# A gated cross-attention and feed-forward block: key maxima by differences and relu, and a changed store of keys

## The reference

```python
q = (query @ Wq + bq).reshape(Bq, Sq, H, DK)
k = (key @ Wk + bk).reshape(Bq, Sk, H, DK)
v = (value @ Wv + bv).reshape(Bq, Sk, H, DK)
scores = jnp.einsum('bqhd,bkhd->hbqk', q, k) / np.sqrt(DK)
attn = jax.nn.softmax(scores.reshape(H * Bq, Sq, Sk), axis=0).reshape(H, Bq, Sq, Sk)
out = jnp.einsum('hbqk,bkhd->bqhd', attn, v).reshape(Bq, Sq, H * DK)
...
xq = _act_fake_quant(x, clip_x[0])
gate = jnp.einsum('bsh,ih->bsi', xq, _weight_fake_quant(w_gate))
up = jnp.einsum('bsh,ih->bsi', xq, _weight_fake_quant(w_up))
h = _act_fake_quant(jax.nn.silu(gate) * up, clip_down[0])
return jnp.einsum('bsi,hi->bsh', h, _weight_fake_quant(w_down))
```

## Time and profile before

| what | us |
|---|---|
| median of 3 runs (lowest, highest) | 846.55 (845.84, 848.11) |
| the profiled execution, its own time | 846.44 |
| its span in the trace | 844.6 |
| busy: PE, DVE, ACT, POOL | 737.2, 753.2, 680.6, 468.8 |

### The profile page before, as it was taken

One profiled execution on the slowest core, in us unless ns is written; L12 is line 12 of the kernel. 1 busy time (PEld: TensorE's weight loads), 2 busy tenths in 40 slices (PEclk: granted clock), 3 DMA queues, 4 the chain that ended last, 5 costly groups with the idle time before them and its releaser, 6 DMA issues. The chain is left out here.

```text
span 844.6 us, 19960 instructions
## 1 busy us (share of the span) xinstructions
PE 737.2 (87%) x8129; PEld 446.0 (53%) x8151; DVE 753.2 (89%) x735; ACT 680.6 (81%) x1094; POOL 468.8 (55%) x210
## 2 busy tenths in 40 slices
PE   8898897787777769999999999999999999469977
PEld 6564372111212125676767777777677678424344
DVE  4799738999999978999999999999999995749957
ACT  3454449999999979898999999999999925759873
POOL 1233454000000010999999999999999996414500
PEclk9999999999999989999999999999999999879989
DMA  9774489999997627678867786878877894000014
GB/s 291 235 230 132 143 194 249 277 256 276 253 253 169 236 74 238 181 203 272 267 185 218 247 294 201 231 212 279 252 207 206 253 300 139 0 2 1 1 50 150
DMA packets 94987, 165.88 MB, mean 196 GB/s; under 512 B 10160, under 2 KB 37552, under 8 KB 94384
## 3 DMA queue, kind: packets, MB, share of 16 engines
q1 hardware_dynamic: 94896, 164.60, 67.3%
HBM read 142.81 MB, written 42.73 MB: 220 GB/s over the span
## 5 line engine op out<-in xcount | busy, mean ns | idle before, releaser
L1030 POOL TENSOR_TENSOR e<-e,recip 128x2048 f32<-128x2048 f32 (+2 forms) x113 | 361.4, 3238 | 22.0 <-DVE recip L1063 21.9
L980 ACT ACTIVATE e<-psY 128x512 f32<-128x512 f32 x512 | 296.1, 645 | 30.5 <-PE psY L912 26.0
L1050 DVE TENSOR_REDUCE partial<-e 128x128 f32<-128x4096 f32 (+1 forms) x80 | 279.4, 3559 | 7.1 <-ACT e L980 7.1
L912 PE MATMUL psY<-arena 128*128 128x128 bf16 x2048 | 200.6, 221 | 0.8 <-DMA arena<-k_stack 0.8
L912 PEld LDWEIGHTS psY<-arena 128*128 128x128 bf16 x2048 | 149.2, 98 | 74.6 <-issue 26.3
L707 ACT ACTIVATE copies<-ps_max 128x1024 bf16<-128x1024 f32 x189 | 175.4, 1084 | 0.1
L908 PE MATMUL psY<-shift,minus 128*128 128x512 bf16 x396 | 152.9, 386 | 11.4 <-PEq L641 5.5
L723 DVE TENSOR_TENSOR high<-copies,high 128x3072 bf16<-128x3072 bf16 x63 | 109.9, 1745 | 0.4 <-ACT copies L707 0.4
L1019 POOL MEMSET ones_w<- 96x128 bf16 x1 | 0.2, 207 | 172.6 <-POOLq L641 172.6
L929 PE MATMUL psX<-e,arena 128*32 128x128 f32 x2048 | 75.9, 288 | 4.0 <-issue 1.9
L718 DVE TENSOR_TENSOR high<-ps_max,high 128x1024 bf16<-128x1024 f32 x63 | 76.4, 1213 | 1.5 <-PE ps_max L686 1.5
(11 more groups left out here) (170 smaller groups left out, 1003.4 us busy)
## 6 DMA issues: line engine op xcount, KB each, us to landing
arena<-k_stack SPq DMA_DIRECT2D x264, 256.0 KB, 3.4
arena<-q_stack SPq DMA_DIRECT2D x64, 256.0 KB, 4.3
arena<-in_x_dram SPq DMA_DIRECT2D x8, 1024.0 KB, 10.0
k_stack<-parts SPq DMA_DIRECT2D x24, 256.0 KB, 3.1
q_stack<-parts SPq DMA_DIRECT2D x24, 256.0 KB, 3.1
k_stack<-k_stack SPq DMA_DIRECT2D x4, 1536.0 KB, 20.6
q_stack<-q_stack SPq DMA_DIRECT2D x4, 1536.0 KB, 17.1
arena<-in_ctx_dram SPq DMA_DIRECT2D x4, 1024.0 KB, 5.8
```

Source lines behind the costliest of these rows:

```text
L912: last = nc.tensor.matmul(bank[:, j * P:(j + 1) * P], ks[:, i % KRING, b * P:(b + 1) * P], qs[:, h, b * P:(b + 1) * P], start=False, stop= ...
L980: nc.scalar.activation(e_at(p, half * HB, (half + 1) * HB).rearrange("p q z i -> p z q i"), ps[n % SCORES][:].rearrange("p (z q i) -> p z ...
L1030: nc.gpsimd.tensor_tensor(part, part, by_pairs(recip[:, r % 2, :], share), ALU.mult).then_inc(pool_scaled, 1)
L1050: nc.vector.tensor_reduce(partial[:, :, k, :], e[:, t:t + n].rearrange("p t q z i -> p q i t z"), AX.XY, ALU.add).then_inc(sum_done, 1)
```

## The change

- **Two heads in one product.** The weights and biases of the odd heads' keys get a minus sign (`permute` with signs; on DVE a column `sign` made from `ident`, multiplied into `bk_s`), so that keys of odd heads lie in DRAM negated. A mixed key tile holds the even head's rows above and the negated odd head's below for chunks 0 to 2: one product with the couple's query tile is the difference of the two heads' scores. A group is now one sequence of one couple, again 64 in all. For chunks 0 to 2 ACT takes the relu of the difference (`gain`), and PE computes minus the odd score minus that, which is minus the larger of the two (`ps_y`). DVE takes the minimum of it over all groups straight into `lowest`, 512 and 1024 columns. Chunk 3 stays as it was: two products (`ps_c`), a copy by ACT, and one merge of 1024 columns a group on DVE.
- **Keys in DRAM.** `k_stack` has 5 rows; SyncE writes all five from the parts (three in the last chunk, where one copy makes the others). The copies of keys are gone. A key tile of `attend` is rows 0 to 3 and rows 1 to 4, in two transfers of 128 KB.
- **Loads.** `load_couple` loads both heads of a couple in 14 transfers; for the first couple all 14 stand ahead of the last writes of `prepare`.
- **`attend`**: the matmul of the maximum takes `plus` for even heads and `minus` for odd; the exponential of odd heads has scale -1/4.
- **`ffn`**: item 42 of 44 goes from POOL to DVE. In down, block 0 is rounded, clipped and multiplied by token tiles, `row` is computed behind the clips, and the last block leaves in three pieces, its last tile in another PSUM slot.

```diff
-K_WRITTEN = (0, 1, 2)
+K_WRITTEN = (0, 1, 2, 3, 4)
+K_AT_LAST = (0, 1, 2)
...
-WRITES = len(K_WRITTEN)
-K_COPIED = (((3, 6), (0, 3)), ((6, 8), (0, 2)))
...
+def load_keys(sp, k_stack, kc, h, tile, loaded):
+    at = 0
+    for first, n in K_READ:
+        sp.dma_start(tile[at:at + n * DK], k_stack[kc, h, first * DK:(first + n) * DK, :]).then_inc(loaded, 16)
...
-    if odd is not None:
-        rows(odd[HALF:P], k_stack, 2 * p + 1, K_MAX_ROWS)
+    rows(mixed[0:HALF], k_stack, 2 * p, K_MAX_ROWS)
+    rows(mixed[HALF:P], k_stack, 2 * p + 1, K_MAX_ROWS, NC - 1)
+    for j in range(2):
+        rows(both[j * HALF:(j + 1) * HALF], q_stack, 2 * p + j, Q_MAX_ROWS)
+    rows(odd[HALF:P], k_stack, 2 * p + 1, K_MAX_ROWS)
...
+            c, g = u // GROUPS, u % GROUPS
+            if group(c, g)[0]:
+                return Q_WRITTEN
+            return K_WRITTEN if c < NC - 1 else K_AT_LAST
...
-                        stack, written = ((k_stack, K_WRITTEN), (q_stack, Q_WRITTEN))[m]
+                        stack = (k_stack, q_stack)[m]
                         h0 = dc * (H // DC)
-                        for part, r in enumerate(written):
...
                     act.wait_ge(s[loaded], 16)
-                    nc.scalar.activation(w_p[:].rearrange("p c (e d h) -> p (c e) d h", e=DC, d=DK),
-                                         w_s[:].rearrange("p c (e h d) -> p (c e) d h", e=DC, d=DK),
-                                         ACT.Copy).then_inc(s["w_permuted"], 1)
-                permute(wk_p, wk_s, "wk_loaded")
+                    step = len(signs)
...
+                nc.vector.tensor_reduce(sign[:, 0:1], ident[:, 1:P:2], AX.X, ALU.max).then_inc(s["sign_set"], 1)
+                dve.wait_ge(s["sign_set"], 1)
+                nc.vector.tensor_scalar(sign[:, 1:2], sign[:, 0:1], -2.0, 1.0, ALU.mult, ALU.add
+                                        ).then_inc(s["sign_set"], 1)
...
+                nc.vector.tensor_scalar(bk_s[:], bk_s[:], sign[:, 1:2], None, ALU.mult).then_inc(s["bias_signed"], 1)
...
+        gain = es.enter_context(nc.sbuf_tensor("gain", [P, RING, MIXED, S], BF16))
+        copies = es.enter_context(nc.sbuf_tensor("copies", [P, RING, 2, 2, S], BF16))
...
+        ps_x = es.enter_context(nc.psum_tensor("ps_x", [P, MIXED, S], F32))
+        ps_y = es.enter_context(nc.psum_tensor("ps_y", [P, MIXED, S], F32))
+        ps_c = es.enter_context(nc.psum_tensor("ps_c", [P, 2, S], F32))
...
+                        sp.wait_ge(y_scored, MIXED * B * (p - 1))
...
+                        load_couple(sp, p, k_stack, q_stack, k_mixed[p % 2], k_odd[p % 2], q_pair[p % 2], loaded[p % 2])
...
+                copy_last_keys(sp, k_stack, keep["k_copied"])
...
+                    for kc in range(MIXED):
+                        if g:
+                            pe.wait_ge(gained, 2 * (g - 1) + (2 if kc == MIXED - 1 else 1))
+                        nc.tensor.matmul(ps_x[:, kc, :], keys(k_mixed, g, kc), queries(g), start=True, stop=True
+                                         ).then_inc(x_scored, 1)
...
+                    if g:
+                        pe.wait_ge(c_copied, g)
+                    for j, tile in enumerate((k_mixed, k_odd)):
+                        last_mm = nc.tensor.matmul(ps_c[:, j, :], keys(tile, g, MIXED), queries(g), start=True, stop=True)
+                    last_mm.then_inc(c_scored, 1)
...
+                    for kc in range(MIXED):
+                        if g:
+                            pe.wait_ge(y_merged, 2 * (g - 1) + (1 if kc == 0 else 2))
+                        nc.tensor.matmul(ps_y[:, kc, :], keys(k_odd, g, kc), queries(g), start=True, stop=False)
+                        pe.wait_ge(gained, 2 * g + (2 if kc == MIXED - 1 else 1))
+                        nc.tensor.matmul(ps_y[:, kc, :], minus[:], gain[:, g % RING, kc, :], start=False, stop=True
+                                         ).then_inc(y_scored, 1)
+                for g in range(GROUPS):
+                    differences(g)
+                    plain(g)
+                    if g:
+                        smaller(g - 1)
+                smaller(GROUPS - 1)
...
+                for g in range(GROUPS):
+                    if g >= RING:
+                        act.wait_ge(y_scored, MIXED * (g - RING + 1))
+                    for k0, k1 in ((0, MIXED - 1), (MIXED - 1, MIXED)):
+                        act.wait_ge(x_scored, MIXED * g + k1)
+                        nc.scalar.activation(gain[:, g % RING, k0:k1, :], ps_x[:, k0:k1, :], ACT.Relu
+                                             ).then_inc(gained, 1)
...
+                    act.wait_ge(c_scored, g + 1)
+                    if g % 2 == 0 and g // 2 > RING:
+                        act.wait_ge(c_merged, 2 * (g // 2 - RING))
+                    dst = copies[:, g // 2 % RING, :, g % 2, :] if g >= 2 else last[:, :, g, :]
+                    nc.scalar.activation(dst, ps_c[:], ACT.Copy).then_inc(c_copied, 1)
...
+                    if j == 0:
+                        dve.wait_ge(c_copied, 2 * m + 2)
+                    if m > 1:
+                        dve.wait_ge(c_merged, 2 * (m - 2) + j + 1)
+                    nc.vector.tensor_tensor(last[:, j], copies[:, m % RING, j], last[:, j], (ALU.max, ALU.min)[j]
+                                            ).then_inc(c_merged, 1)
...
+                    for n, (k0, k1) in enumerate(((0, 1), (1, MIXED))):
+                        dve.wait_ge(y_scored, MIXED * g + k1)
+                        if g:
+                            dve.wait_ge(y_merged, 2 * (g - 1) + n + 1)
+                            nc.vector.tensor_tensor(lowest[:, k0:k1, :], ps_y[:, k0:k1, :], lowest[:, k0:k1, :], ALU.min
+                                                    ).then_inc(y_merged, 1)
...
+                    if g > 2:
+                        merge((g - 1) // 2, (g - 1) % 2)
+                merge(GROUPS // 2 - 1, 1)
...
+                dve.wait_ge(c_merged, merges)
+                for j, op in enumerate((ALU.max, ALU.min)):
+                    nc.vector.tensor_tensor(folds[:, j, :], last[:, j, 0, :], last[:, j, 1, :], op).then_inc(c_merged, 1)
+                dve.wait_ge(c_merged, merges + 2)
+                nc.vector.scalar_tensor_tensor(out=lowest[:, MIXED, :], in0=folds[:, 0, :], scalar=-1.0, in1=folds[:, 1, :],
+                                               op0=ALU.mult, op1=ALU.min).then_inc(folded, 1)
...
                         nxt = (i + KRING) % STEPS
-                        sp.dma_start(ks[:, nxt % KRING, :], k_stack[nxt // H, nxt % H]
-                                     ).then_inc(k_loaded[nxt % KRING], 16)
...
                     else:
-                        nc.tensor.matmul(bank[:], minus[:], shift_at(qc, kc).to_broadcast([P, HB, P]),
...
-                                ACT.Exp, scale=DK ** -0.5).then_inc(exped, 1)
+                                ACT.Exp, scale=(DK ** -0.5, -DK ** -0.5)[half // 2]).then_inc(exped, 1)
...
-                return k % PAIR_ITEMS in POOL_I
+                return k % PAIR_ITEMS in POOL_I and k != ITEMS - 2
...
...
+            def place(n, t0, t1):
+                slot = LAST_SLOT if n == NB - 1 and t0 == TB - 1 else n % 4
+                return psD[:, slot, t0 * D:t1 * D]
+            ENDS = ((0, 2), (2, 3), (3, 4))
...
-                    for n in range(NB):
+                    for t in range(TB):
+                        nc.scalar.activation(hi[:, 0:IC, tokens(t)], hs[:, 0:IC, tokens(t)], ACT.Copy,
+                                             scale=h_scale[:, 2:3]).then_inc(s["h_rounded"], 1)
...
+                    for t in range(TB):
+                        dve.wait_ge(s["h_rounded"], t + 1)
+                        nc.vector.tensor_scalar(hq[:, 0:IC, tokens(t)], hi[:, 0:IC, tokens(t)], -QMAX - 1.0, QMAX,
+                                                ALU.max, ALU.min).then_inc(s["hq_ready"], 1)
+                    nc.vector.tensor_scalar(row[:], wd_row[:], h_scale[:, 1:2], tanh_g[:, 1:2], ALU.mult, ALU.mult
+                                            ).then_inc(row_ready, 1)
...
+                    for part, (t0, t1) in enumerate(ENDS):
+                        scaled(NB - 1, part, t0, t1)
+                        summed(NB - 1, part, t0, t1)
...
+                            if t + 1 == TB or n == NB - 1 and t:
+                                last.then_inc(s["down_ready"], 1)
```

More of the change, by code:

```diff
@@ L142, in prepare @@
         ident = sb("ident", [P, P])
-        ident_b = sb("ident_b", [P, P], BF16)
+        ident_b = keep["plus"]
+        sign = sb("sign", [P, 2])
         diag = sb("diag", [P, DC, P])
@@ L230, in v_turn, with rows_written, writes @@
             return B // 2 + i // 2 if c == 1 and i % 2 else None
+        def rows_written(u):
+            c, g = u // GROUPS, u % GROUPS
+            if group(c, g)[0]:
+                return Q_WRITTEN
+            return K_WRITTEN if c < NC - 1 else K_AT_LAST
+        def writes(i, u):
```

(29 more changed lines are left out.)

259 lines of the change are left out of this document (112 added, 147 removed).

## The result

The changed kernel takes **870.62 us** (median of 4 runs, 870.51 to 874.03) against 847.21 for the kernel before in the same comparison: ratio 1.031, 95% interval 1.028 to 1.035. It is slower by 23 us. The forecast was 830.6 with a range of 824.5 to 842.0, so it had the sign wrong.

A forecast was written before the change was run, and what follows sets the result against it. Bounds: ACT and DVE full in `maxima`; DVE, PE and POOL nearly full in `attend`; PE busiest in down. 846.44 + 3.0 + 1.0 + 0.3 - 19.5 + 0.5 + 0.1 - 1.3 = 830.5, median 830.6; range 824.5 to 842.

The forecast's parts named there:

- The key tile in two transfers: In `attend`: same 256 KB a tile, second transfer issued at least 0.32 later, a few more late tiles; +0.5 us, 0 to +8.
- the allowance: In `attend`: four steps of 5.87 us less about 1 while the tile is scored leave 4.87 for a key tile.
- the landing: In `attend`: key tiles landed in 2.4 to 5.7 us, median 3.3; 3.3 + 0.4 stays below the allowed 4.87.
- Rival 2: Key halves slow `attend`, running one after the other at a lower rate: 838 or 864 us in total; chance 0.06.
- The group of 2.47: In `maxima`: waits among PE, ACT and DVE set a group's period at 2.47 us (2.40 to 2.60), saving 19.5.
- the +1.0 of the clock: Start of `maxima`: PE idles some 3 us, then runs at a low granted clock; +1.0 us, 0 to 2.
- the "no cost" of the DMA in `maxima`: In `maxima`: a couple's loads and copies need 13.4 to 15.4 us against 19.8 available, so no cost.
- 0.93 on ACT against 1.13 on DVE: In `maxima`: 1024 f32 columns from PSUM are quicker on ACT; relus on DVE would cost some 100 us.
- End of `prepare`, +3.0: End of `prepare`: four more loads, 0.917 MB, ahead of the last three writes on SyncE's queue; +3.0 us, 2.5 to 5.
- 0.3: In `prepare`: the keys' sign, more and smaller ACT copies, and 12 more key writes of 256 KB; +0.3 us, 0 to 1.5.
- `ffn` and down: Item 42 on DVE and `row` off the path, +0.1 us; down's earlier first product and shorter end, -1.3 (0 to -2).
- -0.5: End of down: the last scale, add (0.69) and write are halves; -0.5 us.

The follow-up runs named there:

- lower half alone: Changed kernel loading only the lower half of each key tile in `attend`, one transfer of 64 partitions, 128 KB (scores not the reference's): 826.50 us.
- lower half and 8 KB to 128 partitions: Changed kernel loading only each key tile's lower half in `attend`, less its last 32 columns, plus a second transfer of 8 KB to all 128 partitions: 845.78 us.
- lower half and 4 KB to 64 partitions: Changed kernel loading only each key tile's lower half in `attend`, plus a second transfer of 4 KB to the upper 64 partitions: 865.97 us.
- before, halves: Kernel before with one edit: each `attend` key tile loaded in two transfers of 64 partitions and 128 KB, from its old eight rows: 893.91 us, ratio 1.056.
- Neighbouring tiles in one transfer: Changed kernel, lower halves of two neighbouring `attend` key tiles in one transfer, upper halves in a second: 911.52 us, ratio 1.077.
- eight rows: Changed kernel with eight key rows in DRAM, one 256 KB transfer a tile, five DRAM copies in `maxima` for rows not written: 833.00 us, ratio 0.984.

## Why the prediction was wrong

**The key tile in two transfers: the step that failed.** It was priced +0.5 (0 to +8) and measured +46.1. The terms, taken from the times of scoring, issue and landing of each tile in the traces (means over the steps from the 13th on; column halves are the kernel before with two transfers of 128 partitions):

| us | before | column halves | after |
|---|---|---|---|
| tile scored to first issue | 0.04 | 0.22 | 0.83 |
| first to second issue | - | 0.43 | 0.64 |
| last issue to landed | 3.45 | 3.33 | 3.51 |
| scored to landed | 3.49 | 3.98 | 4.99 |

I had the allowance right: 4.87, and in the trace of before the next tile was needed 4.97 after the scoring. I had the landing right too. What I took from the earlier trace rows was the issue time of 0.32 of a transfer to 128 partitions, "at least", without a range for it, and I added it once for a single tile. The real issue takes 0.60, and the next one starts 0.64 after it.

Two tiles come free together every 2.93 (a pair), so SyncE needs 4 x 0.64 = 2.56 for them. The chunk's 8 stores of sums and 16 loads of queries, at about 0.5 each over 32 pairs, are 0.38 more: 2.94, all of the period. Before, it was 2 x 0.32 + 0.38, a third of it. The prediction never made this sum for SyncE. A queue with no slack is late after every disturbance, which is the 0.83; without stores and queries, in the first three rounds, the 2.56 fit, and the rounds kept their pace.

The sum can be read from the traces directly: the durations of all of SyncE's issues in `attend`, divided by the 128 pairs, beside what the stage lost against the kernel before.

| kernel | SyncE's issues, us a pair | `attend` longer by |
|---|---|---|
| before | 0.98 | - |
| lower half alone | 1.37 | 0.5 |
| before, column halves | 2.02 | 8.4 |
| lower half and 8 KB to 128 partitions | 2.58 | 16.0 |
| lower half and 4 KB to 64 partitions | 2.94 | 40.6 |
| after | 2.94 | 46.1 |
| before, halves | 2.95 | 49.7 |

The loss follows this sum and becomes large where it reaches the period of 2.93. Neighbouring tiles in one transfer (1.61, and 85.5 lost) stand outside: there the landing and the later request are the cause.

Rival 2 had the place, the sign and the threshold (4.87, measured 4.99 in the mean), at a chance of 0.06. Its mechanism was not the one that acted, and its formula does not give the size: 63 x (4.99 - 4.87) = 7.6 us, not 46. The Trainium skill ("SBUF — State Buffer", Can I just issue two DMAs to hit both halves?) says that two such transfers serialize; from its fit and its table I had estimated 0.6 more for a tile. The trace agrees with the size of it: the second of two halves landed 3.51 after its issue in the mean, a half alone 2.92. But the run with 4 KB in the second transfer lost 40 us all the same, and the column halves, with the landing of 3.33, only 8.4.

**The group of 2.47: right.** Measured 2.37 and 2.56 by turns, 4.93 for two groups where the chain was added up to 4.87. The stage saved 16.3, and the forecast for this stretch is 18.5 (-19.5 and the +1.0 of the clock). Between the first relu and the last group's lie 157.2 us in 63 periods, which at 2.47 would be 155.6. One period, at the start of the second couple, whose loads were late, took 4.57, 2.1 too long: the "no cost" of the DMA in `maxima` was wrong by that. Start and tail outside 62 periods took 12.4 where I had 10.7, with the low clock in it. One trace does not make this exact: four other kernels with the same code for this stage took 167.5 to 170.8, the longest with two late periods (5.46 and 4.06).

The prediction's 0.93 on ACT against 1.13 on DVE compares a copy with a maximum of two inputs. In the changed kernel DVE has two operations with one input from PSUM, of 512 and 1024 columns in 0.69 and 1.23 (L787), where ACT's relu of 1024 takes 1.02; so the order holds for like operations too.

**End of `prepare`, +3.0: right in sign, high in size, and hidden in the pair of profiled executions.** The same code ends this stage at one of two times. Three operations on DVE take 0.9 to 1.0 us each more in some traces. From two kernels with the old code for this stage (before, then the halves in it), two of the three, and POOL beside the last:

```profile
88.21 2.50 DVE L568 TENSOR_SCALAR wrq<-wrow 128x1280 bf16<-128x1280 f32 x2
92.29 1.84 DVE L568 TENSOR_SCALAR arena<-arena 128x1408 bf16<-128x1408 f32 x1
92.11 1.27 POOL L304 TENSOR_TENSOR parts<-rest,parts 128x512 bf16<-128x512 f32 x1 [2.08 <-ACT parts L448]
```
```profile
87.28 1.54 DVE L568 TENSOR_SCALAR wrq<-wrow 128x1280 bf16<-128x1280 f32 x2
90.40 0.88 DVE L568 TENSOR_SCALAR arena<-arena 128x1408 bf16<-128x1408 f32 x1
90.57 1.72 POOL L304 TENSOR_TENSOR parts<-rest,parts 128x512 bf16<-128x512 f32 x1 [0.73 <-ACT parts L448]
```

The difference goes with the order of DVE and POOL. In all seven traces that have the long ones, all three start while a `parts` operation of POOL is running (92.29 within 92.11 to 93.38) and end 0.4 to 0.8 after it. The short ones start before POOL's, which then takes 1.4 to 1.7 instead of 1.2, or in its last 0.15 us, or beside none. Which comes first differs between traces of the same code; what decides it is not shown.

| first product of `maxima` | old loads | new loads |
|---|---|---|
| long (2.50 and 1.84) | 126.56, 126.56 | 127.87, 128.60, 128.96, 129.07, 129.63 |
| short (1.54 and 0.88) | 123.24 | 124.56, 124.63, 125.36, 126.86 |

Within a row the new order ends the stage 1.3 to 3.6 later, 2.2 in the mean, where the forecast was 3.0 and 0.3; as predicted, SyncE's last writes land last (it waited 9.5 for them, 7.1 before). Between the rows lie 3.3 (old) and 3.5 in the mean (new). The changed kernel's profile fell in the lower row and that of before in the upper; hence -2.0. The same difference may stand behind part of the spread of one kernel's times, such as the 829.85 to 838.06 above; only one execution of each was traced, so that is not shown.

**The clock.** After 4.2 us of idle PE the granted clock at the first products of `maxima` was 0.58 over 3.5 us, most of it at the lower of the two levels (1.2 GHz), as expected; the +1.0 is inside the stage's 167.1.

```profile
124.50:128.00 3.50, 3.32 (x8) 0.81 (x8) 0.00 (x0) 2.40 (x4) 3.43 (x2) 0.58 0.81 267
```

**`ffn` and down, -1.2 in all: right in sign, forecast too small.** Down's first product stands 2.5 us behind the block's first (3.7 before), which I had priced; the tail from the last product's start fell from 5.6 to 4.4, -1.2 instead of -0.5 (the last add takes 0.42 instead of 0.69); the block gave 3.05 in all. The other 0.7 before it is within the spread of that stretch, with `row` (0.41) gone from it. Other traces weaken these shares: the block took 38.4 with the old code in two and 36.9 in the third (column halves), and 35.3 to 35.7 in all nine with the new, whether its first product stood 1.5 or 2.5 behind the start. So it gave 1.3 to 3.1, and the early first product is not shown to be what paid.

```profile
866.17 0.42 DVE L1637 TENSOR_TENSOR xn<-xn,x 128x256 f32<-128x256 f32 x1
```

Put together, without the halves the changed kernel takes 826.5 (half tiles) to 833.0 (eight rows), about the forecast of 830.6. That is in part luck: in the traces `maxima` gave 2.2 less than forecast, and `ffn` with down 2.6 more. One step, off by 46 us, turned the sign.

## What to carry to other kernels

Treat the engine that issues DMAs as an engine with a budget: add up its issues over the period of the loop that it feeds, with all stores and other loads, and compare the sum with the period, before looking at how long a transfer takes to land. Do not take the issue time of one shape for another; a transfer that is cut in two may cost nearly four times the queue time, as here (0.32 to 2 x 0.60). When a stage differs between two profiled executions, look at a third with the same code for this stage before giving it to an edit, and at whether two engines' operations have changed their order.

## What the runs showed of the hardware

- The issue of a DMA from SyncE's queue took 0.32 us for 128 partitions of 2 KB, 0.45 for 64 partitions when alone, and 0.60 for each of two such in a row, whether the second held 128 KB or 4 KB. A second one of 128 partitions and 1 KB behind another of its kind took 0.43.
- A source pattern of 2 x 64 overlapping rows for a tile of 128 partitions took 4.9 us to issue in the median, and a tile came every 5.3 us in the mean (1365.3 us of `attend` for 256). Its semaphore got 3 updates a transfer instead of 16.
- 256 KB to 64 partitions landed in 4.0 us (median), 128 KB to 64 in 3.0 (2.6 without a second behind it), 256 KB to 128 in 3.3.
- The same scalings of f32 to bf16 on DVE took 0.88 or 1.84, and two of them 1.54 or 2.50, from one trace to another. The long ones started while a POOL operation was running, the short ones before one, in its last 0.15 us or beside none, and the end of the stage moved by 3.3 to 3.5 us.
- 1024 columns of f32 from PSUM to bf16 took 1.02 us as a relu on ACT and 1.23 as a copy on DVE (changed kernel).
